# Attention of the second layer: VectorE's low parts of the probabilities, moved between the two row maxima of a step

## The reference, cut to what matters

```
Q = (q @ Wq.T + bq) ... 16 heads of 16 features, B = 4, 512 queries, 512 keys
scores = einsum('bhqd,bhkd->bhqk', Q, K) / sqrt(16)
scores = where(mask == 1, -1e9, scores)
attn = softmax(scores)
out = einsum('bhqk,bhkd->bhqd', attn, V)
out @ Wo.T + bo
```

## Time and profile before

| | |
|---|---|
| median of 3 runs | 1317.81 us (1317.72 to 1319.56) |
| profiled execution, its own time | 1319.14 us |
| its span | 1317.4 us |
| mean granted clock of TensorE | 0.953 of full |
| PE busy | 1167.9 us (89%) |
| DVE busy | 879.4 us (67%) |
| ACT busy | 697.0 us (53%) |

### The profile page before, as it was taken

The page is one execution under the profiler, slowest core; times in us unless marked ns, Lnnn a source line. Parts: engine busy times, 40 slices in busy tenths (PEclk is TensorE's granted clock), DMA queues, the critical chain, the costliest instruction groups (busy, mean ns, idle before and its releaser), DMA issues. The chain is left out here.

```text
span 1317.4 us, 20464 instructions
## 1 busy us (share of the span) xinstructions
PE 1167.9 (89%) x6928; PEld 1014.4 (77%) x6928; DVE 879.4 (67%) x1669; ACT 697.0 (53%) x1053; POOL 337.8 (26%) x347
## 2 busy tenths in 40 slices
PE   3888769988879979969999999999999999978988
PEld 2666647877768969969999988778788788767877
DVE  6787765556645635635665454799999989976565
ACT  2222214655533424424444233798888988976655
POOL 2400018212123500410320025432342432332020
PEclk9888879988889989989999999999999999998999
DMA  8100001002217253252222013322421423310001
GB/s 294 64 0 0 0 8 64 1 5 68 61 48 157 65 152 96 73 144 92 93 96 89 1 40 97 102 66 73 128 64 52 139 70 103 88 38 6 14 21 48
DMA packets 66852, 92.83 MB, mean 70 GB/s; under 512 B 15440, under 2 KB 32592, under 8 KB 66640
## 3 DMA queue, kind: packets, MB, share of 16 engines
q1 hardware_dynamic: 65152, 89.67, 23.1%
q10 hardware_dynamic: 1616, 2.10, 0.5%
HBM read 80.45 MB, written 11.14 MB: 70 GB/s over the span
## 5 line engine op out<-in xcount | busy, mean ns | idle before, releaser
L1823 DVE CUSTOM_DVE_ANT_0 at_pr<-at_sc,at_mk 128x512 f32<-128x512 f32 x256 | 165.5, 684 | 24.8 <-PE at_sc L2054 24.3
L1725 ACT ACTIVATE at_pr<-at_pr,at_nmx 128x512 f32<-128x512 f32 x256 | 170.4, 716 | 21.4 <-DVE at_nmx L1823 20.7
L1969 DVE TENSOR_TENSOR W_1l<-at_pt,W_1h 128x1024 fp32r<-128x1024 f32 x128 | 155.8, 1217 | 5.5 <-ACT W_1h L1720 5.2
L2069 PE MATMUL at_pt<-ident,at_pr 128*128 128x128 f32 x1024 | 135.9, 276 | 21.1 <-DVE W_1l L1969 20.4
L2069 PEld LDWEIGHTS at_pt<-ident,at_pr 128*128 128x128 f32 x1024 | 115.5, 142 | 44.5 <-issue 25.2
L1720 ACT ACTIVATE W_1h<-at_pt 128x1024 fp32r<-128x1024 f32 x128 | 130.8, 1022 | 34.5 <-PE at_o L2088 33.1
L315 DVE TENSOR_TENSOR moe_ms<-moe_hs,moe_gate 128x512 f32<-128x512 f32 x112 | 86.2, 770 | 89.9 <-ACT moe_hs L282 56.6
L282 ACT ACTIVATE moe_hs<-moe_hid,cols 128x512 f32<-128x512 f32 x128 | 88.1, 688 | 104.0 <-PE moe_hid L167 103.0
L274 ACT ACTIVATE moe_hh<-moe_ms 128x512 fp32r<-128x512 f32 x112 | 70.8, 632 | 133.4 <-DVE moe_ms L315 133.4
L301 DVE TENSOR_TENSOR moe_hl<-moe_ms,moe_hh 128x512 fp32r<-128x512 f32 x112 | 87.9, 785 | 69.2 <-ACT moe_hh L274 69.2
L2088 PE MATMUL at_o<-W_1h,at_vaug 128*128 128x512 f32 x256 | 113.7, 444 | 0.3 <-DVE W_1l L1969 0.3
(11 more groups left out here) (314 smaller groups left out, 3293.6 us busy)
## 6 DMA issues: line engine op xcount, KB each, us to landing
moe_gate<-expert_weights SPq DMA_DIRECT2D x224, 128.0 KB, 2.9
w_stage<-in_ew SPq DMA_DIRECT2D x8, 1024.0 KB, 6.3
at_kp<-at_heads SPq DMA_DIRECT2D x96, 64.0 KB, 2.7
at_qp<-at_heads SPq DMA_DIRECT2D x96, 64.0 KB, 2.8
w_stage<-in_w SPq DMA_DIRECT2D x4, 1024.0 KB, 9.8
f_gate<-expert_weights SPq DMA_DIRECT2D x32, 128.0 KB, 2.9
w_stage<-in_mask SPq DMA_DIRECT2D x16, 256.0 KB, 3.6
at_rb<-at_recip SPq DMA_DIRECT2D x64, 64.0 KB, 2.0
```

Source lines behind the costliest of these rows:

```text
L1725: act.activation(pr_of(t)[:, x, :], pr_of(t)[:, x, :], ACT.Exp, bias=nmx[:, t % 4, x:x + 1], scale=-1.0).then_inc(s["ex"], 1)
L1823: dve.tensor_tensor_reduce(pr_of(t)[:, x, :], SB[x][:, :], mk[u // 2 % 2][:, j, :], -float(HD) ** -0.5, 3.0e38, ALU.add, ALU.min, nmx[:, t ...
L1969: dve.tensor_tensor(PH[1][:, n % 2, :], PT[n % 2][:, :, :].rearrange("p c q -> p (c q)"), f(PH[0][:, n % 2, :]), ALU.subtract).then_inc(s[ ...
L2069: last = pe.transpose(PT[t % 2][:, c, j * P:(j + 1) * P], pr_of(t - i + j // 2)[:, j % 2, kc * P:(kc + 1) * P], g.ident[:, :])
```

## The change

In every step with a low part to make, it moves that instruction with its two waits from behind both maxima and most of the extra work to between the first and the second maximum. Nothing is added or removed, and no semaphore count changes.

```
                     if 0 <= u < UNITS:
                         score_max(t, 0)
+                    if 0 <= n < STEPS * UNITS:
+                        dve.wait_ge(s["ph"], n + 1)
+                        if n >= 2:
+                            dve.wait_ge(s["pv"], n - 1)
+                        dve.tensor_tensor(PH[1][:, n % 2, :], PT[n % 2][:, :, :].rearrange("p c q -> p (c q)"),
+                                          f(PH[0][:, n % 2, :]), ALU.subtract).then_inc(s["pl"], 1)
+                    if 0 <= u < UNITS:
                         score_max(t, 1)
                     if st == 0 and u >= 2:
                         add_y(2 * (u - 2) + 1)
...
                     if st == 14 and u >= 1:
                         add_y(2 * (u - 1))
-                    if 0 <= n < STEPS * UNITS:
-                        dve.wait_ge(s["ph"], n + 1)
-                        if n >= 2:
-                            dve.wait_ge(s["pv"], n - 1)
-                        dve.tensor_tensor(PH[1][:, n % 2, :], PT[n % 2][:, :, :].rearrange("p c q -> p (c q)"),
-                                          f(PH[0][:, n % 2, :]), ALU.subtract).then_inc(s["pl"], 1)
                     if st == 0 and u % 2 == 0 and nxt < B:
```

## The result

The changed kernel takes 1424.99 us (median of 4 runs, 1420.62 to 1432.02), the kernel before 1317.76 in the same comparison: a ratio of 1.083, 95% interval 1.079 to 1.087. The forecast was 1423. The profiled execution took 1423.06 us, its span is 1421.3 us, 103.9 more than before.

What follows compares the result with a forecast made beforehand. VectorE's own work was taken to bound the kernel, 93% busy. With the change, 112 x 3.53 = 395.4, + 39.2 + 4 = 438.6 us against 333, +105.6, gave 1423 us; 80% range 1396 to 1458.

Steps and rivals of the forecast that it cites:

- The trip: Loop of low part, second maximum, second exponential, high part, next low part, closing within one step: 3.53 us, 112 times.
- ScalarE's extra work: Instructions between the second exponential and the next high part, 72 in the stretch, said to add 39.2 us.
- VectorE's extra work: Work behind the second maximum, up to 1.1 us free per step; only norm-statistics and weights' low-part steps cost, 4 us.
- TensorE's clock: Granted clock in the stretch of 112 steps, said to stay at 1.00 with TensorE 73% busy; no term.
- The row of the prediction: Profile window from 1164 to 1176 us, TensorE 74% busy at clock 1.00, taken as evidence the clock stays up.
- the second rival: TensorE's clock swings to 1.2 GHz in a third to half of 128 steps: 77 to 115 us more, 1500 to 1538; 9%.
- The sum: The 112 steps from first to 113th low part: 438.6 us where they take 333 now, +105.6.
- The last 15 steps: Steps of unit 7 behind the 113th low part, about 4.2 us each: 0 change, between -5 and +10 us.

Runs made afterwards that it cites:

- low_first: Low part moved ahead of both maxima of its step, where the changed kernel has it between them: 1492.3 us.
- exp_later: The changed kernel with ScalarE issuing the second exponential of a step one step later, behind the next step's high part: 1368.8 us.
- its control: The kernel before, in its old VectorE order, with ScalarE's second exponential issued one step later: 1358.8 us.
- low_after_both: Low part right behind both maxima and ahead of the extra work, where the changed kernel has it between the maxima: 1317.6 us.
- The added copies: One more unused small copy per step of units 0 to 6: in the changed kernel 1458.7 us on ScalarE, 1433.2 on VectorE; in the kernel before 1327.5 and 1337.7.
- low_odd_steps: The kernel before with the low part moved between the two maxima in odd steps only: 1364.3 us.
- low_fourth_steps: The kernel before with the low part moved between the maxima only in steps 1, 5, 9 and 13 of a unit: 1341.3 us.
- act_extra_early: The changed kernel with ScalarE's extra work of units 0 to 6 moved from behind both exponentials to ahead of them: 1398.9 us.
- dve_more_after: The changed kernel with one more unused small VectorE copy behind the second maximum in each step of units 0 to 6: 1433.2 us.
- low_early_last: The kernel before with the low part right behind both maxima in unit 7 only: 1302.9 us, ratio 0.989.

## Why the prediction was right

- **The trip.** Right in mechanism and size: 3.53 us forecast, 3.53 measured in most plain steps, and nearly the same term by term (1.14 + 0.69 + 0.03 + 0.63 + 1.01 + 0.03 in the trip shown above). low_first (a longer trip), exp_later with its control (the trip cut on ScalarE) and low_after_both (cut on VectorE) show it from three sides.
- **ScalarE's extra work adds in full**, 39.2 us: right, and about 38.5 when the steps of the changed kernel are added up. The stretch has 70 such instructions, not 72, and each makes its step longer by its length less 0.10 us: 4.02 to 4.11 for a short one, 4.48 for the one of 1.05 us, 4.90 for the one of 1.47. The added copies say the same, with 0.30 us for one of 0.40.
- **VectorE's extra work is covered**, 4 us: right, 4.2 by the same sum. The three steps of the stretch with norm statistics took 4.77 us (forecast about 4.8, and four of them), the one with the weights' low parts 5.09. The added copies cost nothing in 90 of 109 steps.
- **TensorE's clock**, no term, and a forecast of 1.00: small, but not nothing. The granted clock over the stretch is 0.96, with TensorE busy for 357 of 443 us. The row of the prediction, 12 us at 74% busy and full clock, did not carry over to this stretch. The clock fell ten times in the stretch. Nine of these falls follow a single wait of 1.44 to 2.37 us, one a wait of 1.25; but 17 other waits of over 1.4 us were followed by none, so the length of the wait alone doesn't decide it. Timeline of TensorE in the changed kernel:

```profile
1027.37 0.50 PE L2055 MATMUL at_sc<-at_kp,at_qp 128*128 128x512 f32 x1 [1.46 <-DVE at_nmx L1823]
...
1030.12 1.91 PE L2070 MATMUL at_pt<-ident,at_pr 128*128 128x128 f32 x8
```

  Eight transposes took 1.91 us, at 1.2 GHz, where they take 1.03 to 1.04 at 2.4; the next first maximum was late by 2.03 us, and the step took 4.75 us where its like took 4.11. Five steps (unit 2 st 2, units 3, 4 and 6 st 4, unit 5 st 6, with 4.80, 4.75, 4.73, 4.76 and 5.22 us) exceed their likes by 4.1 us together, and each of the five stands beside a fall of the clock. Two more falls stand beside steps that are 0.3 and 0.1 us too long, which makes 4.6 us; the others cost nothing that a step shows, since most of a fall hides in the 1.1 us that the first maximum has to spare.
  The Trainium skill ("TensorE: Matmul & The Clock Gate", section "A second HAM failure mode: psum-queue depth-cycling") says that short idle times between groups of matmuls can make the clock swing between its two levels. The trace agrees that it swings, but with 4.6 us of loss against the 77 to 115 of the second rival.
- **The sum**: 395.4 + 39.2 + 4 + 0 = 438.6 us forecast; 395.4 + about 38.5 + 4.2 + 4.6 = 442.7 measured. Only the clock was missing from it.
- **The last 15 steps**, 0 in a range of -5 to +10: +2.7.
- **The close hit of the total is partly luck**: 110.0 + 2.7 us of loss in the trace for 105.6 forecast, against 8.8 us less in parts that the change doesn't touch. By medians the loss is 107.2. The prediction's remark that a measurement tells 0.2% from no change was too hopeful: its interval is 0.4% either way, and the kernel before scatters by 1.3% over the comparisons.
- Outside the forecast itself, my expectations missed clearly three times: low_odd_steps, where I followed the trip through VectorE's queue and not through ScalarE's, and exp_later with its control, where I gave the cure no price of its own. By 3 to 7 us they missed in low_fourth_steps, act_extra_early, dve_more_after and low_early_last.

## What to carry to other kernels

Before an instruction that waits is moved ahead of another, follow what stands behind it now: on its own engine, then through that result's consumer on the other engine, and through that engine's queue back to the wait. If the trip closes in one step instead of two, its full length is the step's floor, however idle the engines are. Idle time on an engine is no room for extra work if the place where the work goes lies inside such a trip, as it did here between the second exponential and the high part on ScalarE; put it where the trip doesn't pass, here behind the second maximum on VectorE.

## What the runs showed that I had not expected

An order that is best for the body of a loop can be wrong for its last turn: one place for the low part was 9 us worse in 112 steps and 6.7 us better in the last 15. The total time of one kernel scattered by more than 1% between comparisons (before: 1307 to 1325 us), while the 112 steps repeated far better: between before and low_early_last, which have the same order in units 0 to 6, 107 of the 112 differ by at most 0.02 us. Differences under 10 us could be read in the trace and hardly in the medians.
